# One-hot-like embedding products on one core: the x ring cut into 20 tiles, and loads of up to four tiles

## The chip, the core and the metric

One Trainium2 chip, one of its cores. The kernel is a single launch; the host only transposes and pads x, pads w and puts the output in order. The metric is device time in microseconds (us), the median of repeated runs. x is 104 MB of float32 and has to be read once, so bytes and the rate of the DMA engines are the first thing to look at.

## The reference

Ten tables, each a matrix product with a sparse x (float32, nearly all zeros, ones elsewhere), and a sum of them:

```python
VOCABS = [12500, 6250, 2500, 1250, 625, 250, 1000, 500, 200, 100]   # batch 1024, dim 64
embs = [jnp.dot(x, w) for x, w in zip(xs, ws)]
emb_sum = sum(embs)
q_emb = sum(jnp.dot(x ** 2, w ** 2) for x, w in zip(xs, ws))
fm_ans = 0.5 * (emb_sum ** 2 - q_emb)
return jnp.concatenate([fm_ans] + embs, axis=-1)
```

## The kernel before

A *tile* is 128 rows of the vocabulary by 1024 columns of the batch (512 KB). Partition p of a table holds consecutive rows of its vocabulary, so n neighbouring tiles are n x 4096 consecutive bytes of HBM for every partition, and n x 4096 bytes of SBUF. The last tile of a table (its *tail*) lies elsewhere and is loaded by itself. There are 203 tiles.

Tiles are worked through in *chunks* of one or two (`ORDER`, 108 chunks, numbered `k`), and chunks belong to *groups* of up to eight tiles (31 groups, numbered `g`), which share one load of weights. The tables come in the order 8, 9, 5, 4, 7, 3, 2, 1, 0, 6; tables 1 and 0 (49 and 98 tiles) are most of the work, and in them a group is four chunks of two tiles.

Each engine has its own instruction list, written out by hand, with semaphores between them:

- SP (`block.sync`) issues the loads of x into a ring of 8 slots (`SLOTS`) of two tiles each. The load of chunk k first waits until both readers have finished chunk k - 8 (`ones_counted` and `set_counted`). After the last x load it issues the stores of the results.
- DVE (`count_ones`) compares each chunk with 1 and counts the hits; nothing but a final check depends on the counts, but they hold the slot. Between chunks it adds a finished table's sums to `total` (`add(n)`, five chunks after the table's end), and that needs ACT's `copy_emb(n)`.
- ACT (`count_set`) makes `is_set`, the sign of each element, which is the matrix that TensorE multiplies, and counts as well. In the same list stand `load_w(g+3)`, a DMA of weights on ACT's own queue, issued in group g behind its second chunk; `square(g+2)`, which waits for those weights to land, behind the third chunk; and `copy_sums` and `copy_emb` for finished tables.
- POOL splits the weights into a high and a low part; PE multiplies each tile by both.

A weights load is 128 rows of up to 2048 bytes. Where a group holds the tail of a table whose tail is short (tables 8, 3, 2, 1, 0, 6), it is two or three DMAs, the extra ones with rows of 256 bytes.

Of the kernel before, what the change touches and what calls it, by code (L numbers as in the profile page):

```python
# [5 lines left out]
ALU = mybir.AluOpType  # L6
ACT = mybir.ActivationFunctionType
F32 = mybir.dt.float32
# [5 lines left out]
P = 128  # L14
D = 64
# [25 lines left out]
CHUNK = max(FULL)  # L41
GROUP = sum(FULL)

SLOTS = 8
SETS = 5

WHOLES = 3
# [8 lines left out]
class Chunk:  # L56


    def __init__(self, k, table, tile, n, at):
        self.k, self.table, self.tile, self.n, self.at = k, table, tile, n, at  # L60
        self.slot, self.turn = k % SLOTS, k // SLOTS
        self.tail = tile + n == TILES[table]

        self.rows = TAIL[table] if TILES[table] == 1 else P
        self.group = None


class Group:
# [31 lines left out]
NGROUPS, NCHUNKS = len(GROUPS), len(CHUNKS)  # L100


G_ORDER = [9] + [t for t in range(NT) if t != 9]
BEGIN = [min(g.chunks[0].k for g in GROUPS if g.place == n) for n in range(NT)]
END = [max(g.end for g in GROUPS if g.place == n) for n in range(NT)]
# [11 lines left out]
def rec_kernel(nc, xs, ws, out):  # L117
# [5 lines left out]
    with ExitStack() as ctx:  # L123
        def sb(name, shape, dt):
            return ctx.enter_context(nc.sbuf_tensor(name, shape, dt))
# [5 lines left out]

        sums = ctx.enter_context(nc.psum_tensor("sums", [P, NB, 512], F32))

        x_ring = sb("x_ring", [P, SLOTS * CHUNK * BATCH], F32)

        is_set = [sb(f"is_set{i}", [P, CHUNK * BATCH], F32R) for i in range(SETS)]
        is_one = [sb(f"is_one{i}", [P, CHUNK * BATCH], U8) for i in range(2)]
# [20 lines left out]
        g_weights = sb("g_weights", [P, 2, D], F32)  # L158

        w_landed = [sem(f"w_landed{i}") for i in range(WHOLES)]  # L160
        x_landed = [sem(f"x_landed{s}") for s in range(SLOTS)]
# [30 lines left out]

        block = ctx.enter_context(nc.Block())

        def in_slot(slot, elements):
            at = slot * CHUNK * BATCH
            return x_ring[:, at:at + elements]

        def x_of(chunk):
            return in_slot(chunk.slot, chunk.n * BATCH)[0:chunk.rows]  # L200

        def part_of(group, part):

# [13 lines left out]

        @block.sync
        def _(sp):
            for chunk in CHUNKS:  # L220
                if chunk.k >= SLOTS:

                    sp.wait_ge(ones_counted, chunk.k - SLOTS + 1)
                    sp.wait_ge(set_counted, chunk.k - SLOTS + 1)
                at = chunk.tile * BATCH
                sp.dma_start(x_of(chunk),
                             x_end[chunk.table] if chunk.tail else
                             x_dram[chunk.table][:, at:at + chunk.n * BATCH]
                             ).then_inc(x_landed[chunk.slot], 16)

            for n, (t, _) in enumerate(ORDER[:-1]):
                sp.wait_ge(emb_copied, n + 1)
                sp.dma_start(out[t + 1], results[:, t + 1, :, :]).then_inc(stored, 16)
            sp.wait_ge(fm_ready, 1)
            sp.dma_start(out[0], results[:, 0, :, :]).then_inc(stored, 16)
            sp.wait_ge(flag_ready, 1)
            odd = sp.value_load(odd_flag[0:1, 0:1], min_val=0, max_val=FLAG_MAX)
            sp.wait_ge(stored, 16 * (NT + 1))
            with sp.If(odd != 0):
                base = zeros = 0  # L240
                for t in G_ORDER:
                    end, rows = TILES[t] - 1, TAIL[t]
                    if end:
                        with sp.Fori(0, end) as i:

                            sp.wait_ge(g_multiplied, base + i + 1)
                            sp.dma_start(in_slot(0, BATCH), x_dram[t][:, bass.ds(i * BATCH, BATCH)]
                                         ).then_inc(gx_landed, 16)
# [3 lines left out]
                    sp.dma_start(in_slot(0, BATCH)[0:x_end[t].shape[0]], x_end[t]).then_inc(gx_landed, 16)  # L252
# [15 lines left out]
        def _(act):  # L268
# [20 lines left out]
                nc.scalar.activation(w[:, 1], w[:, 0], ACT.Square).then_inc(squared, 1)  # L289

            def count_set(chunk):
                act.wait_ge(x_landed[chunk.slot], 16 * (chunk.turn + 1))
                if chunk.k >= SETS:

                    act.wait_ge(x_multiplied, chunk.k - SETS + 1)
                nc.scalar.activation(  # L296
                    is_set[chunk.k % SETS][0:chunk.rows, 0:chunk.n * BATCH],
                    x_of(chunk).bitcast(U32), ACT.Sign,
                    accum_out=set_counts[0:chunk.rows, chunk.k:chunk.k + 1]).then_inc(set_counted, 1)
# [71 lines left out]
        def _(pe):  # L371
# [49 lines left out]
            with pe.If(odd != 0):  # L421
                with pe.Fori(0, sum(TILES)) as i:
                    pe.wait_ge(gx_landed, 16 * (i + 1))
                    pe.wait_ge(gw_landed, 16 * (i + 1))
                    pe.wait_ge(gx_ready, 2 * (i + 1))
                    for b in range(NB):
                        block_b = slice(b * P, (b + 1) * P)
                        nc.tensor.matmul(sums[:, b, 0:D], in_slot(0, BATCH)[:, block_b],
                                         g_weights[:, 0, :], start=True, stop=True,
                                         skip_group_check=True)  # L430
                        last = nc.tensor.matmul(sums[:, b, D:2 * D], in_slot(1, BATCH)[:, block_b],
                                                g_weights[:, 1, :], start=False, stop=True,
                                                skip_group_check=True)
                    last.then_inc(g_multiplied, 1)
# [3 lines left out]
        def _(dve):  # L438
# [4 lines left out]
            dve.wait_ge(constants, 4)  # L443

            def count_ones(chunk):
                dve.wait_ge(x_landed[chunk.slot], 16 * (chunk.turn + 1))
                if chunk.k >= 2:

                    dve.wait_ge(ones_counted, chunk.k - 1)
# [48 lines left out]
            with dve.If(odd != 0):  # L498
# [7 lines left out]
                dve.wait_ge(stored, 16 * (NT + 1))  # L506
                dve.wait_ge(x_multiplied, NCHUNKS)

                g_link(nc.vector.memset(in_slot(0, BATCH), 0.0))
                nc.vector.nop().then_inc(g_multiplied, 1)  # L510
                g_link(nc.vector.memset(total[:, :, :, :], 0.0))
                base = 0
                for t in G_ORDER:
# [3 lines left out]
                    def add_tile(i):  # L517
                        dve.wait_ge(gx_landed, 16 * (base + i + 1))
                        dve.wait_ge(gw_landed, 16 * (base + i + 1))
                        x, w = in_slot(0, BATCH), g_weights[:, 0, :]  # L520
                        nc.vector.tensor_tensor(in_slot(1, BATCH), x, x, ALU.mult
                                                ).then_inc(gx_ready, 1)
                        nc.vector.tensor_tensor(g_weights[:, 1, :], w, w, ALU.mult).then_inc(gx_ready, 1)
                        dve.wait_ge(g_multiplied, base + i + 2)
# [39 lines left out]
```

## Time and profile before

| | |
|---|---|
| time, median of 3 runs | 285.73 us (285.54 to 285.94) |
| the profiled execution's own time | 285.67 us |
| its span in the trace | 283.9 us |
| granted TensorE clock, mean | 0.987 |
| DVE busy | 240.3 us (85%) |
| ACT busy | 227.6 us (80%) |
| PE busy | 218.4 us (77%) |
| bytes moved by DMA | 113.88 MB, mean 401 GB/s |

The span runs from the first to the last instruction of the trace; 1.8 us of the measured time lie around it. Shares of busy time are averages over the whole span. "DMA share" in the trace is the mean busy share of the core's 16 DMA engines.

### The profile page before, as it was taken

How to read it: one execution, taken by the hardware profiler on the slowest of the kernel's cores; microseconds unless marked ns; L12 is line 12 of the kernel's file. 1: busy time of each engine (PE TensorE's matmuls, PEld its weight loads, DVE VectorE, ACT ScalarE, POOL GpSimd, SP SyncE). 2: the span in 40 equal slices, each digit the busy share in tenths (PEclk: the TensorE clock that was granted, in tenths of full speed). 3: DMA queues.
4: the chain of work that ended last, by engine and by line, in shares of the span. 5: the costliest groups of instructions: out<-in, count | busy, mean ns of one | idle time of the engine just before them, and what ended most of it. 6: DMA issues, size and time to landing. Idle time of an engine off the chain costs nothing.

```text
span 283.9 us, 2928 instructions
## 1 busy us (share of the span) xinstructions
PE 218.4 (77%) x878; PEld 154.2 (54%) x878; DVE 240.3 (85%) x236; ACT 227.6 (80%) x271; POOL 88.1 (31%) x68
## 2 busy tenths in 40 slices
PE   0459989998887878888687778778778778777791
PEld 0338657776565655555465555555555555545561
DVE  3752999999999989988789988988988988888874
ACT  0769999999978878878887877877877878778762
POOL 0432427317234124107244044044044044004000
PEclk9998999999999999999999999999999999999997
DMA  7999999999999999999999999999999999999972
GB/s 234 396 404 415 407 417 415 420 413 418 416 422 418 419 423 413 419 417 420 413 421 415 420 421 417 421 423 414 418 422 419 416 418 415 418 413 420 410 304 99
DMA packets 22417, 113.88 MB, mean 401 GB/s; under 512 B 3728, under 2 KB 4752, under 8 KB 10752
## 3 DMA queue, kind: packets, MB, share of 16 engines
q1 hardware_dynamic: 16976, 106.90, 91.5%
q10 hardware_dynamic: 5424, 6.79, 6.7%
q8 instruction: 7, 0.11, 0.2%
q14 instruction: 10, 0.08, 0.1%
HBM read 110.79 MB, written 2.88 MB: 400 GB/s over the span
## 4 chain that ended last, share of the span: by engine, by line
DMA 63%; issue 23%; DVE 6%; ACT 3%; PE 2%; POOL 1%; ACTq 1%; DVEq 0%; POOLq 0%
DMA x_ring<-in_x_dram 58%; DVE is_one L450 5%; DMA whole<-in_w_dram 5%; ACT is_set L296 2%; PE sums L385 1%; ACT turned L307 1%; POOL low L366 1%; PE sums L392 1%; DVE total L487 0%; ACT whole L289 0%; ACTq L276 0%; POOL high L364 0%; DVE results L490 0%; DVE results L493 0%; ACTq L283 0%
## 5 line engine op out<-in xcount | busy, mean ns | idle before, releaser
L450 DVE TENSOR_SCALAR_CACHE_REDUCE is_one<-x_ring 128x2048 uint8<-128x2048 f32 (+2 forms) x108 | 226.2, 2114 | 29.0 <-DMA x_ring<-in_x_dram 28.8
L296 ACT ACTIVATE is_set<-x_ring 128x2048 fp32r<-128x2048 uint32 (+2 forms) x108 | 192.2, 1784 | 37.2 <-DMA x_ring<-in_x_dram 37.1
L385 PE MATMUL sums<-is_set,low 128*128 128x512 f32 x398 | 134.8, 420 | 59.6 <-ACT is_set L296 52.7
L385 PE MATMUL sums<-is_set,high 128*128 128x512 f32 x398 | 125.9, 398 | 0.0
L385 PEld LDWEIGHTS sums<-is_set,low 128*128 128x128 f32 x398 | 68.4, 191 | 104.2 <-ACT is_set L296 54.3
L385 PEld LDWEIGHTS sums<-is_set,high 128*128 128x128 f32 x398 | 75.9, 191 | 17.5
L364 POOL CAST high<-whole 128x1024 fp32r<-128x1024 f32 (+5 forms) x31 | 27.0, 871 | 170.5 <-ACT whole L289 170.5
L366 POOL TENSOR_TENSOR low<-whole,high 128x1024 fp32r<-128x1024 f32 (+5 forms) x31 | 60.6, 1953 | 2.5
L296 ACT ACTIVATION_READ_ACCUMULATOR is_set<-x_ring 128x1 f32 (+1 forms) x108 | 20.7, 192 | 0.0
L289 ACT ACTIVATE whole<-whole 128x512 f32<-128x512 f32 (+5 forms) x31 | 16.8, 541 | 4.1 <-DMA whole<-in_w_dram 4.1
L392 PE MATMUL sums<-identity,turned 128*128 128x128 f32 x80 | 11.2, 286 | 0.8 <-ACT turned L337 0.8
L392 PEld LDWEIGHTS sums<-identity,turned 128*128 128x128 f32 x80 | 10.1, 150 | 2.6 <-issue 1.4
L462 DVE TENSOR_TENSOR total<-sums,total 128x1024 f32<-128x1024 f32 x8 | 9.7, 1219 | 1.7 <-ACT results L312 1.7
L307 ACT ACTIVATE turned<-sums 128x1024 f32<-128x1024 f32 x9 | 9.2, 1018 | 0.0
L450 DVE DVE_READ_ACCUMULATOR is_one<-x_ring 128x1 f32 (+1 forms) x108 | 8.8, 81 | 0.0
L459 DVE COPY total<-sums 128x1024 f32<-128x1024 f32 x1 | 1.2, 1225 | 8.2 <-ACT results L312 8.2
L289 ACT ACT_TABLE_LOAD x1 | 1.3, 1283 | 7.7 <-DMA whole<-in_w_dram 7.7
L312 ACT ACTIVATE results<-sums 128x512 f32<-128x512 f32 x9 | 5.4, 601 | 1.0 <-PE sums L392 1.0
L337 ACT ACTIVATE turned<-sums 128x512 f32<-128x512 f32 x2 | 1.1, 596 | 1.2 <-PE sums L385 1.2
L487 DVE TENSOR_TENSOR total<-sums,total 128x512 f32<-128x512 f32 x2 | 1.3, 685 | 0.9 <-PE sums L392 0.9
L342 ACT ACTIVATE results<-sums 128x256 f32<-128x256 f32 x2 | 0.8, 383 | 1.3 <-DVE total L487 1.3
L439 DVE MEMSET ones<- 128x128 f32 x1 | 0.2, 165 | 0.9 <-PEq L547 0.9
(17 smaller groups left out, 3.7 us busy)
## 6 DMA issues: line engine op xcount, KB each, us to landing
x_ring<-in_x_dram SPq DMA_DIRECT2D x91, 1024.0 KB, 18.3
x_ring<-in_x_dram SPq DMA_DIRECT2D x16, 512.0 KB, 10.2
whole<-in_w_dram ACTq DMA_DIRECT2D x19, 256.0 KB, 7.5
out_dram<-results SPq DMA_DIRECT2D x10, 256.0 KB, 12.4
x_ring<-in_x_dram SPq DMA_DIRECT2D x1, 448.0 KB, 6.5
whole<-in_w_dram ACTq DMA_DIRECT2D x2, 192.0 KB, 5.7
whole<-in_w_dram ACTq DMA_DIRECT2D x2, 160.0 KB, 7.2
out_dram<-results ACTq DMA_DIRECT2D x1, 256.0 KB, 2.1
```

The costliest lines, as they stand in the source:

```text
L289: nc.scalar.activation(w[:, 1], w[:, 0], ACT.Square).then_inc(squared, 1)
L296: nc.scalar.activation(is_set[chunk.k % SETS][0:chunk.rows, 0:chunk.n * BATCH], x_of(chunk).bitcast(U32), ACT.Sign, accum_out=set_counts[0 ...
L307: nc.scalar.activation(turned[n % 2][:, :].rearrange("p (a b) -> p a b", a=2), sums[:, at:at + 2, :], ACT.Copy).then_inc(sums_copied, 1)
L312: nc.scalar.activation(results[:, t + 1, :, :], turning(n)[:, :, 0, :], ACT.Copy).then_inc(emb_copied, 1)
L364: nc.gpsimd.tensor_copy(upper, w).then_inc(high_ready, 1)
L366: nc.gpsimd.tensor_tensor(part_of(group, low), w, upper.bitcast(F32), ALU.subtract).then_inc(parts_ready, 1)
L385: last = nc.tensor.matmul(sums[:, summing(n, half), :], w, x[0:chunk.rows, at:at + HALF], start=first, stop=False, skip_group_check=True)
L392: last = nc.tensor.transpose(turning(n)[:, b, :, :], turned[n % 2][:, b * P:(b + 1) * P], identity[:, :])
L450: nc.vector.tensor_scalar(is_one[chunk.k % 2][0:chunk.rows, 0:chunk.n * BATCH], x_of(chunk), 1.0, None, ALU.is_equal, ALU.add, accum_out=o ...
L459: nc.vector.tensor_copy(total[:, :, :, :], turning(n)).then_inc(added, 1)
L462: nc.vector.tensor_tensor(total[:, :, :, :], turning(n), total[:, :, :, :], ALU.add).then_inc(added, 1)
L487: nc.vector.tensor_tensor(total[:, blocks, :, :], turning(n)[:, blocks, :, :], total[:, blocks, :, :], ALU.add).then_inc(added, 1)
```

## The change

The ring becomes 20 tiles (`RING`) without slots, and a *load* becomes a thing of its own (`Load`, `plan_loads`). Neighbouring chunks of one group are joined into one load as long as it has at most four tiles (`LOAD`); a tail stays alone, and so do all chunks of the last table (`LAST`, table 6), whose loads are those of before. The load's place `at` runs around the ring, and jumps to 0 where the load wouldn't fit before the end. It waits (`free`) until the readers have finished every chunk whose place it overwrites. Semaphores for landing are 12 (`LANDS`) instead of 8. The readers still work chunk by chunk; both chunks of a load wait for the same landing. Of 64 loads, 42 have four tiles, 2 have three, 5 have two and 15 have one; before there were 108, 91 of two tiles and 17 of one.

```diff
-SLOTS = 8
+
+LOAD = 4
+RING = 20
+LANDS = 12
...
+def plan_loads():
+    lists = []
+    for group in GROUPS:
+        joined = []
+        for chunk in group.chunks:
+
+            if joined and (chunk.tail or group.table == LAST or sum(c.n for c in joined) + chunk.n > LOAD):
+                lists.append(joined)
+                joined = []
+            joined.append(chunk)
+        lists.append(joined)
+    loads, at = [], 0
+    for i, chunks in enumerate(lists):
+
+        at = 0 if at + sum(chunk.n for chunk in chunks) > RING else at
+        loads.append(Load(i, chunks, at))
+        at += loads[-1].n
+
+        loads[-1].free = max([o.end for o in loads[:-1] if o.at < at and loads[-1].at < o.at + o.n] +
+                             [o.end for o in loads[:-1] if o.land == loads[-1].land] + [0])
+    return loads
...
-        x_ring = sb("x_ring", [P, SLOTS * CHUNK * BATCH], F32)
+        x_ring = sb("x_ring", [P, RING * BATCH], F32)
...
-            for chunk in CHUNKS:
-                if chunk.k >= SLOTS:
-
-                    sp.wait_ge(ones_counted, chunk.k - SLOTS + 1)
-                    sp.wait_ge(set_counted, chunk.k - SLOTS + 1)
-                at = chunk.tile * BATCH
-                sp.dma_start(x_of(chunk),
-                             x_end[chunk.table] if chunk.tail else
-                             x_dram[chunk.table][:, at:at + chunk.n * BATCH]
-                             ).then_inc(x_landed[chunk.slot], 16)
+            free = 0
+            for load in LOADS:
+                if load.free > free:
+
+                    free = load.free
+                    sp.wait_ge(ones_counted, free)
+                    sp.wait_ge(set_counted, free)
+                at = load.tile * BATCH
+                sp.dma_start(in_ring(load.at, load.n)[0:load.rows],
+                             x_end[load.table] if load.tail else
+                             x_dram[load.table][:, at:at + load.n * BATCH]
+                             ).then_inc(x_landed[load.land], 16)
...
-                act.wait_ge(x_landed[chunk.slot], 16 * (chunk.turn + 1))
+                act.wait_ge(x_landed[chunk.load.land], 16 * (chunk.load.turn + 1))
...
-                dve.wait_ge(x_landed[chunk.slot], 16 * (chunk.turn + 1))
+                dve.wait_ge(x_landed[chunk.load.land], 16 * (chunk.load.turn + 1))
```

Only SP's list gets other instructions; the lists of ACT, DVE, PE and POOL keep theirs in the same order, with other landings to wait for.

SP's list at the start, before (in_x8 is x of table 8, and so on; 128x1024 is one tile, 128x2048 two; the times at the end count equal rows):

```order
L226 DMA x_ring<-in_x8_dram 128x1024 x2
L226 DMA x_ring<-in_x9_dram 112x1024
L226 DMA x_ring<-in_x5_dram 128x1024 x2
L226 DMA x_ring<-in_x4_dram 128x2048 x2
L226 DMA x_ring<-in_x4_dram 128x1024
L226 DMA x_ring<-in_x7_dram 128x2048 [waits set_counted,ones_counted]
L226 DMA x_ring<-in_x7_dram 128x1024 [waits set_counted,ones_counted] x2
```

The same place of the change:

```order
L268 DMA x_ring<-in_x8_dram 128x1024 x2
L268 DMA x_ring<-in_x9_dram 112x1024
L268 DMA x_ring<-in_x5_dram 128x1024 x2
L268 DMA x_ring<-in_x4_dram 128x4096
L268 DMA x_ring<-in_x4_dram 128x1024
L268 DMA x_ring<-in_x7_dram 128x3072
L268 DMA x_ring<-in_x7_dram 128x1024
L268 DMA x_ring<-in_x3_dram 128x4096
L268 DMA x_ring<-in_x3_dram 128x2048
L268 DMA x_ring<-in_x3_dram 128x3072 [waits set_counted,ones_counted]
```

Before, ten tiles are issued ahead of the first wait; now it is twenty, in eleven loads.

SP's list from table 2 to the end, before:

```order
L226 DMA x_ring<-in_x2_dram 128x2048 [waits set_counted,ones_counted] x9
L226 DMA x_ring<-in_x2_dram 128x1024 [waits set_counted,ones_counted] x2
L226 DMA x_ring<-in_x1_dram 128x2048 [waits set_counted,ones_counted] x24
L226 DMA x_ring<-in_x1_dram 128x1024 [waits set_counted,ones_counted]
L226 DMA x_ring<-in_x0_dram 128x2048 [waits set_counted,ones_counted] x48
L226 DMA x_ring<-in_x0_dram 128x1024 [waits set_counted,ones_counted] x2
L226 DMA x_ring<-in_x6_dram 128x2048 [waits set_counted,ones_counted] x3
L226 DMA x_ring<-in_x6_dram 128x1024 [waits set_counted,ones_counted] x2
```

And from table 1 to the end in the change:

```order
L268 DMA x_ring<-in_x1_dram 128x4096 [waits set_counted,ones_counted] x7
L268 DMA x_ring<-in_x1_dram 128x4096
L268 DMA x_ring<-in_x1_dram 128x4096 [waits set_counted,ones_counted] x4
L268 DMA x_ring<-in_x1_dram 128x1024 [waits set_counted,ones_counted]
L268 DMA x_ring<-in_x0_dram 128x4096 [waits set_counted,ones_counted] x24
L268 DMA x_ring<-in_x0_dram 128x1024 [waits set_counted,ones_counted]
L268 DMA x_ring<-in_x0_dram 128x1024
L268 DMA x_ring<-in_x6_dram 128x2048
L268 DMA x_ring<-in_x6_dram 128x2048 [waits set_counted,ones_counted]
L268 DMA x_ring<-in_x6_dram 128x2048
```

The 72 loads of two tiles of tables 1 and 0 have become 36 of four; the last table's are the same.

## Rows read from the trace of the kernel before

**Rows 1.** The page's second part: 40 equal slices of 7.1 us.

```profile
DMA  7999999999999999999999999999999999999972
GB/s 234 396 404 415 407 417 415 420 413 418 416 422 418 419 423 413 419 417 420 413 421 415 420 421 417 421 423 414 418 422 419 416 418 415 418 413 420 410 304 99
DMA packets 22417, 113.88 MB, mean 401 GB/s; under 512 B 3728, under 2 KB 4752, under 8 KB 10752
```

**Rows 2.** DMA queues (q1 SP's, q10 ACT's): packets, MB, share of 16 engines' span.

```profile
q1 hardware_dynamic: 16976, 106.90, 91.5%
q10 hardware_dynamic: 5424, 6.79, 6.7%
```

**Rows 3.** Windows: us, busy of PE, PEld, DVE, ACT, POOL, clock, DMA share, GB/s.

```profile
168.00:172.00 4.00, 3.01 (x12) 2.22 (x13) 3.62 (x5) 3.04 (x5) 0.00 (x0) 1.00 1.02 424
204.00:208.00 4.00, 3.16 (x13) 1.94 (x11) 3.54 (x3) 3.77 (x5) 1.98 (x2) 1.00 1.02 414
```

**Rows 4.** The page's groups: the two readers of x_ring.

```profile
L450 DVE TENSOR_SCALAR_CACHE_REDUCE is_one<-x_ring 128x2048 uint8<-128x2048 f32 (+2 forms) x108 | 226.2, 2114 | 29.0 <-DMA x_ring<-in_x_dram 28.8
L296 ACT ACTIVATE is_set<-x_ring 128x2048 fp32r<-128x2048 uint32 (+2 forms) x108 | 192.2, 1784 | 37.2 <-DMA x_ring<-in_x_dram 37.1
```

**Rows 5.** DMA issues: count, KB each, median us from issue to landing.

```profile
x_ring<-in_x_dram SPq DMA_DIRECT2D x91, 1024.0 KB, 18.3
whole<-in_w_dram ACTq DMA_DIRECT2D x19, 256.0 KB, 7.5
...
whole<-in_w_dram ACTq DMA_DIRECT2D x3, 28.0 KB, 9.1
```

**Rows 6.** Timeline of ACT in tables 0 and 6: start, us, what.

```profile
158.40 0.33 ACTq L276 DMA_DIRECT2D whole<-in_w_dram  x1
...
173.41 0.62 ACT L289 ACTIVATE whole<-whole 128x512 f32<-128x512 f32 x1
...
243.01 0.35 ACTq L276 DMA_DIRECT2D whole<-in_w_dram  x1
...
258.14 0.62 ACT L289 ACTIVATE whole<-whole 128x512 f32<-128x512 f32 x1
```

**Rows 7.** Timeline of ACT at the start: square(3) and its weights load, copy_emb(0).

```profile
10.65 0.33 ACTq L276 DMA_DIRECT2D whole<-in_w_dram  x1
...
17.00 0.47 ACT L289 ACTIVATE whole<-whole 128x320 f32<-128x320 f32 x1 [3.67 <-DMA whole<-in_w_dram]
...
26.26 0.59 ACT L312 ACTIVATE results<-sums 128x512 f32<-128x512 f32 x1
```

**Rows 8.** Timeline of DVE: add(0), and the chunk behind k = 22.

```profile
26.88 1.23 DVE L459 COPY total<-sums 128x1024 f32<-128x1024 f32 x1 [8.25 <-ACT results L312]
...
63.65 2.27 DVE L450 TENSOR_SCALAR_CACHE_REDUCE is_one<-x_ring 128x2048 uint8<-128x2048 f32 x1
```

**Rows 9.** Timeline of ACT at the end.

```profile
259.67 1.91 ACT L296 ACTIVATE is_set<-x_ring 128x2048 fp32r<-128x2048 uint32 x1 [0.91 <-DMA x_ring<-in_x_dram]
...
261.58 1.04 ACT L296 ACTIVATE is_set<-x_ring 128x1024 fp32r<-128x1024 uint32 x1
...
264.71 1.92 ACT L296 ACTIVATE is_set<-x_ring 128x2048 fp32r<-128x2048 uint32 x1 [0.96 <-DMA x_ring<-in_x_dram]
...
269.11 1.01 ACT L307 ACTIVATE turned<-sums 128x1024 f32<-128x1024 f32 x1
270.01 1.91 ACT L296 ACTIVATE is_set<-x_ring 128x2048 fp32r<-128x2048 uint32 x1
```

**Rows 10.** Timeline of DVE at the end.

```profile
269.68 2.29 DVE L450 TENSOR_SCALAR_CACHE_REDUCE is_one<-x_ring 128x2048 uint8<-128x2048 f32 x1 [0.19 <-DMA x_ring<-in_x_dram]
...
273.03 1.22 DVE L450 TENSOR_SCALAR_CACHE_REDUCE is_one<-x_ring 128x1024 uint8<-128x1024 f32 x1
...
275.71 1.22 DVE L462 TENSOR_TENSOR total<-sums,total 128x1024 f32<-128x1024 f32 x1 [1.45 <-ACT results L312]
```

More of the change, by code:

```diff
@@ L60, in __init__ @@
         self.k, self.table, self.tile, self.n, self.at = k, table, tile, n, at
-        self.slot, self.turn = k % SLOTS, k // SLOTS
         self.tail = tile + n == TILES[table]
         self.rows = TAIL[table] if TILES[table] == 1 else P
-        self.group = None
+        self.group = self.load = None
+class Load:
+    def __init__(self, i, chunks, at):
+        self.chunks, self.at, self.i = chunks, at, i
+        self.table, self.tile, self.tail = chunks[0].table, chunks[0].tile, chunks[0].tail
+        self.n, self.rows = sum(chunk.n for chunk in chunks), chunks[0].rows
+        self.end = chunks[-1].k + 1
+        self.land, self.turn = i % LANDS, i // LANDS
+        for chunk in chunks:
+            chunk.load, chunk.within = self, chunk.tile - self.tile
 class Group:
@@ L100 @@
 NGROUPS, NCHUNKS = len(GROUPS), len(CHUNKS)
+def plan_loads():
[16 more added lines that the diff above has]
+    return loads
+LOADS = plan_loads()
 G_ORDER = [9] + [t for t in range(NT) if t != 9]
@@ L160, in rec_kernel @@
         w_landed = [sem(f"w_landed{i}") for i in range(WHOLES)]
-        x_landed = [sem(f"x_landed{s}") for s in range(SLOTS)]
+        x_landed = [sem(f"x_landed{s}") for s in range(LANDS)]
         x_multiplied = sem("x_multiplied")
@@ L193, in rec_kernel, with in_ring @@
         block = ctx.enter_context(nc.Block())
-        def in_slot(slot, elements):
-            at = slot * CHUNK * BATCH
-            return x_ring[:, at:at + elements]
+        def in_ring(tile, n):
+            return x_ring[:, tile * BATCH:(tile + n) * BATCH]
         def x_of(chunk):
-            return in_slot(chunk.slot, chunk.n * BATCH)[0:chunk.rows]
+            return in_ring(chunk.load.at + chunk.within, chunk.n)[0:chunk.rows]
         def part_of(group, part):
@@ L246, in _ @@
                             sp.wait_ge(g_multiplied, base + i + 1)
-                            sp.dma_start(in_slot(0, BATCH), x_dram[t][:, bass.ds(i * BATCH, BATCH)]
+                            sp.dma_start(in_ring(0, 1), x_dram[t][:, bass.ds(i * BATCH, BATCH)]
                                          ).then_inc(gx_landed, 16)
@@ L251, in _ @@
                     sp.wait_ge(g_multiplied, base + end + 1)
-                    sp.dma_start(in_slot(0, BATCH)[0:x_end[t].shape[0]], x_end[t]).then_inc(gx_landed, 16)
+                    sp.dma_start(in_ring(0, 1)[0:x_end[t].shape[0]], x_end[t]).then_inc(gx_landed, 16)
                     w_end, before = w_dram[t][:, end * D:TILES[t] * D], P - rows if end else 0
@@ L427, in _ @@
                         block_b = slice(b * P, (b + 1) * P)
-                        nc.tensor.matmul(sums[:, b, 0:D], in_slot(0, BATCH)[:, block_b],
+                        nc.tensor.matmul(sums[:, b, 0:D], in_ring(0, 1)[:, block_b],
                                          g_weights[:, 0, :], start=True, stop=True,
                                          skip_group_check=True)
-                        last = nc.tensor.matmul(sums[:, b, D:2 * D], in_slot(1, BATCH)[:, block_b],
+                        last = nc.tensor.matmul(sums[:, b, D:2 * D], in_ring(1, 1)[:, block_b],
                                                 g_weights[:, 1, :], start=False, stop=True,
@@ L507, in _ @@
                 dve.wait_ge(x_multiplied, NCHUNKS)
-                g_link(nc.vector.memset(in_slot(0, BATCH), 0.0))
+                g_link(nc.vector.memset(in_ring(0, 1), 0.0))
                 nc.vector.nop().then_inc(g_multiplied, 1)
@@ L519, in add_tile @@
                         dve.wait_ge(gw_landed, 16 * (base + i + 1))
-                        x, w = in_slot(0, BATCH), g_weights[:, 0, :]
-                        nc.vector.tensor_tensor(in_slot(1, BATCH), x, x, ALU.mult
+                        x, w = in_ring(0, 1), g_weights[:, 0, :]
+                        nc.vector.tensor_tensor(in_ring(1, 1), x, x, ALU.mult
                                                 ).then_inc(gx_ready, 1)
```

## The prediction

> **What bounds the kernel now.** Read the slices first [rows 1]: from the second to the 38th the DMA engines are busy nine tenths or more, at 396 to 423 GB/s. Then the readers [rows 4]: DVE and ACT each sat idle before chunks, 29.0 and 37.2 us in all, and nearly all of it ended with a landing of x. So from about 7 us to about 270 us the DMA engines' rate sets the end, and some 12 us of closing work follow. No engine's busy share matters as long as x keeps streaming. Ahead of it lies a deep queue: a two-tile load lands 18.3 us after its issue [rows 5], though two tiles take only 1,048,576 B / 0.418 MB/us = 2.5 us at the rate of [rows 1].
>
> Two things can move the time: what a byte costs the DMA engines, and whether they ever run dry.
>
> **What a packet costs.** q1 has 16,976 packets [rows 2]. Counted from the code this is one per row and one per engine for each DMA's semaphore: 91 x 128 rows of 8 KB, 16 x 128 + 112 of 4 KB, 10 x 128 of stores, and 118 x 16 for semaphores. So a row of 8 KB is one packet. Solve the two queues for a price per packet a and per megabyte b, in engine-us out of 16 x 283.9 = 4542: q1 gives 16,976 a + 106.90 b = 0.915 x 4542 = 4156, q10 gives 5,424 a + 6.79 b = 0.067 x 4542 = 304. That is b = 37.4 us/MB (26.7 B/ns) and a = 9.2 ns. But the records overlap: the share reads 1.02 where an engine can't be over 1 [rows 3], and 2% of 4542 us over 22,417 packets [rows 1] is 4 ns each. So a packet costs between 5.2 and 9.2 ns beside its bytes.
>
> The change takes away 44 loads (108 less 64) and with each 128 rows and 16 semaphore packets: 44 x 144 = 6,336 packets, the bytes being the same. 6,336 x 5.2 / 16 = 2.1 us; x 9.2 = 3.6 us. I take 6.6 ns, nearer the lower end, since the overlap is real but its 4 ns comes from a share with two decimals: **-2.6 us**. The part of it after table 0 is nothing, so it is all there when the last table begins.
>
> The Trainium skill ("DMA: Bandwidth & Descriptors", Why small descriptors are slow) gives 3 cycles of overhead for each packet, at 850 MHz (same page, Where 436 GB/s comes from) 3.5 ns; by that, an estimate, the saving would be 1.4 us, and the packet's price in the rows is above it.
>
> **What the end costs.** The last load of table 0 before the tail's singles now lands two chunks at once, the earlier of them 2.5 us later than it would alone. Take its landing as time 0 (259.67 before) [rows 9]. The next arrivals are one 2-tile load at +5.04 (264.71), and +7.5 and +10.0 after it (269.68 on DVE) [rows 9, 10]. ACT has from time 0: 1.91 (first chunk), 0.5 (square(30), which stood ahead of the landing at 258.14 [rows 6] and now stands between the two), 1.91, 1.04 + 1.04: it is free at +6.4, not +4.0, so the 0.96 us of idle time before 264.71 is gone and ACT doesn't catch up: +8.3, +10.2, and 0.9 for copy_sums (269.11 to 270.01) gives +11.1 for the start of the third chunk, where before it was +10.34. That is **+0.8 us** on the path through ACT, PE and the closing copies. DVE is later by about 1.1 us (starts lie 0.08 us closer than the recorded 2.29 and 1.22, so two chunks of 2.21, two of 1.14, three of 2.21 and two of 1.14 make 15.6, against 14.5 from 259.67 to the end of its last count at 274.2), but it has 1.45 us of idle time before its add [rows 10]. Bounds: 0.4 if ACT recovers part of it, 1.4 if DVE's lag counts too.
>
> **Does the stream run dry?** SP waits for both readers of what a load overwrites. In table 0 the ring holds five four-tile loads, and the next is issued when the oldest pair of chunks is counted, so 16 tiles less those in work are queued: over 12 us. The tightest place by the plan is the second load of table 1 (load 21), which waits for chunk 22: 48 tiles are issued before it. DVE finishes chunk 22 at 63.65 [rows 8]. By then the first nine slices (63.9 us) have moved 3521 x 7.1 / 1000 = 25.0 MB [rows 1], less some 1.8 MB of weights (54 tiles of 32 KB): 44 tiles. Four tiles, 5 us, are still in the queue, 4 us after the time that a load needs to start. In this stretch both readers are behind (DVE sat 8.25 us before add(0) [rows 8], waiting for ACT's copy_emb(0) at 26.26, which was itself late because square(3) waited 3.67 us for weights [rows 7]). Whatever makes ACT later at the start moves 63.65 by as much. Cost taken: 0, with the cover of 4 us named.
>
> **Weights behind larger packets.** A 256 KB load of weights has 8 rows and a semaphore on each engine and takes 7.5 us [rows 5]; 9 x 0.09 us of its own would be below 1 us, so it alternates with x packets of 8 KB (0.31 us: 8192 B at 26.7 B/ns plus a), 9 x 0.31 = 2.8 us of it. With packets of 16 KB (0.62 us) this adds 2.8 us: 10.3 us. In table 0 it has 173.41 - 158.40 = 15.0 us [rows 6]: covered by 4.7 us. Where the load is three DMAs it has about 19 packets per engine and took 9.1 us [rows 5]: plus 19 x 0.31 = 5.9 makes 15.0, and it has 258.14 - 243.01 = 15.1 [rows 6]. That is the edge; ACT's list reaches load_w a little earlier when two chunks land together, about 2 us, which speaks for no stall. At the start, the load issued at 10.65 landed at 17.0 [rows 7]; at most 9 x 0.31 = 2.8 us more, less than the 4 us of cover. Cost taken: 0, at most 2.
>
> The skill's rule for it ("DMA: Bandwidth & Descriptors", Queues, rings and completion order) is that an engine goes round its queues and switches only at packet boundaries, so larger x packets hold weights up; the 7.5 us agree with alternation. It would turn the sum round only if both covers went, which is the third rival.
>
> **Sum.** 285.67 - 2.6 + 0.8 = **283.9 us**. The profiled execution lies 0.06 us under the median of the runs, so this stands for the median too.
>
> **Rivals.**
>
> 1. *Rows of 16 KB are cut back into packets of 8 KB or cost twice a packet's price.* Then only 44 x 16 semaphore packets go: 704 x 6.6 ns / 16 = 0.3 us. The end's 0.8 stays. 285.67 - 0.3 + 0.8 = **286.2 us**. Against it: a row of 8 KB is one packet where 4 KB rows are too [rows 2]; but no row shows 16 KB. The skill's "DMA: Bandwidth & Descriptors" (SWDGE vs HWDGE vs iDMA) prefers packets of at most 4096 B, which the 8 KB of this trace already exceed.
>
> 2. *The stream runs dry in tables 2 and 1.* ACT is made later at the start by slower weights (2.8 us for each of the loads for groups 3 and 4, some 5.6 together), copy_emb and with it DVE's add follow, chunk 22 is counted at 69 (63.65 + 5.6), load 21 comes some 1.5 us too late, and perhaps one more load as well. 1.5 to 4 us of idle DMA: 283.9 + 1.5 to 4, say **286.6 us**, slower. It decides from an ACT delay of 4 us on. For it: ACT and DVE have no idle time to catch up in here. Against: the x packets beside these first weights are in part 4 KB and 12 KB, and the ring reaches 20 tiles ahead, four to ten more than before at the start.
>
> 3. *Weights late at the table borders* (groups 9, 16, 29, 30): ACT stands 1 to 2 us in square(29) or square(30), shortly before the end, where it has 0.5 to 0.9 us of idle time per chunk to give. **284.9 us**.
>
> 4. *Packets cost the full 9.2 ns and the end nothing*: 285.67 - 3.6 + 0.4 = **282.5 us**.
>
> **How the numbers follow.** 0.2% of 285.7 is 0.57 us, about what a measurement of this kernel can tell. Forecast (282.7 to 284.9): 0.50. Rival 1: 0.18. Rival 2: 0.16. Rival 3: 0.10. Rival 4: 0.06. Faster by over 0.2% means under 285.2: forecast, rival 4 and half of rival 3, 0.61. Within 0.2%: most of rival 1, some of 2 and 3: 0.21. Slower, over 286.3: most of rival 2 and a third of rival 1: 0.18. The range of 282.6 to 286.7 takes in the ends of the packet price and rivals 1 to 3 up to their middles and leaves under 2 in 10 out.
>
> **What would show it.** In the page of the changed kernel: 22,417 - 6,336 = 16,081 packets, if rows of 16 KB are one packet (rival 1: 21,713 if cut in two). A rate of 424 GB/s in weights-free windows [rows 3] should become 427 to 428. The 256 KB weights should land after about 10.3 us. No slice between the second and the 38th should fall under 400 GB/s; a dip near 60 to 70 us is rival 2. At the end ACT should show no idle time before the last table's first chunk. The prediction is wrong if x arrives no faster, or if DMA engines stand idle.

## The result and the profile after

The changed kernel takes **282.47 us** (median of 4 runs, 282.42 to 282.64), the kernel before 285.84 us beside it (4 runs, 285.54 to 286.51). The ratio is 0.988, with a 95% interval of 0.9862 to 0.9898: faster, by 3.4 us. The prediction was 283.9 us with a range of 282.6 to 286.7, so the direction was right, but the time is 1.4 us lower than forecast and lies 0.1 us outside the range.

One number ahead of the prediction is wrong: there are 199 tiles (91 chunks of two and 17 of one), not 203. No step was worked out from it.

The page of the changed kernel, second and third part (slices of 7.0 us), which answer to [rows 1] and [rows 2]:

```profile
span 280.8 us, 2830 instructions
...
DMA  7999999999999999999999999999999999999972
GB/s 226 409 401 421 411 432 422 414 410 428 423 428 425 427 427 421 421 416 435 418 425 422 434 421 427 421 430 416 427 427 418 429 427 420 423 423 406 411 304 94
DMA packets 16080, 113.87 MB, mean 406 GB/s; under 512 B 3024, under 2 KB 4048, under 8 KB 9792
...
q1 hardware_dynamic: 10640, 106.89, 91.0%
```

The bytes are those of before, the packets are 6,337 fewer: a row of 16 KB is one packet. The DMA engines are still busy from the second slice to the 38th, and no slice lies under 400 GB/s. The kernel is bound as before; the same stream has become faster. One window over most of it, us, busy of PE, PEld, DVE, ACT, POOL, clock, DMA share, GB/s, first in the kernel before:

```profile
80.00:250.00 170.00, 135.67 (x522) 92.13 (x520) 150.44 (x133) 138.78 (x149) 53.85 (x35) 1.00 1.02 418
```

and in the changed kernel:

```profile
80.00:250.00 170.00, 134.06 (x537) 94.40 (x536) 149.20 (x134) 136.23 (x152) 55.43 (x35) 1.00 1.01 424
```

418 has become 424 GB/s. The readers' groups and the DMA issues, beside [rows 4, 5]:

```profile
L492 DVE TENSOR_SCALAR_CACHE_REDUCE is_one<-x_ring 128x2048 uint8<-128x2048 f32 (+2 forms) x108 | 223.6, 2115 | 30.5 <-DMA x_ring<-in_x_dram 30.3
...
L338 ACT ACTIVATE is_set<-x_ring 128x2048 fp32r<-128x2048 uint32 (+2 forms) x108 | 191.4, 1775 | 36.7 <-DMA x_ring<-in_x_dram 36.7
...
x_ring<-in_x_dram SPq DMA_DIRECT2D x42, 2048.0 KB, 21.0
...
whole<-in_w_dram ACTq DMA_DIRECT2D x19, 256.0 KB, 9.8
```

Both readers wait as long as before (DVE 29.0 before and 30.5 us now, ACT 37.2 and 36.7), only in fewer and longer pieces, and still for x. Weights land after 9.8 us instead of 7.5. In the waits of ACT (total, times, longest) this comes to almost nothing:

```profile
ACT is_set L338 <- DMA x_ring<-in_x_dram: 36.7, 36, 1.4
...
ACT whole L331 <- DMA whole<-in_w_dram: 4.7, 2, 4.2
```

4.7 us for weights in two waits, both in the early tables; the kernel before had 4.1 in two. Then ACT's timeline at the end, beside [rows 9]:

```profile
255.75 1.91 ACT L338 ACTIVATE is_set<-x_ring 128x2048 fp32r<-128x2048 uint32 x1 [1.39 <-DMA x_ring<-in_x_dram]
...
257.66 0.62 ACT L331 ACTIVATE whole<-whole 128x512 f32<-128x512 f32 x1
258.18 1.90 ACT L338 ACTIVATE is_set<-x_ring 128x2048 fp32r<-128x2048 uint32 x1
...
262.15 1.90 ACT L338 ACTIVATE is_set<-x_ring 128x2048 fp32r<-128x2048 uint32 x1
...
264.05 1.90 ACT L338 ACTIVATE is_set<-x_ring 128x2048 fp32r<-128x2048 uint32 x1
...
265.94 1.01 ACT L349 ACTIVATE turned<-sums 128x1024 f32<-128x1024 f32 x1
266.85 1.90 ACT L338 ACTIVATE is_set<-x_ring 128x2048 fp32r<-128x2048 uint32 x1
```

From the landing of the last pair of table 0 ACT works without a pause to the third chunk of the last table: 266.85 - 255.75 = 11.10 us, the +11.1 of the prediction. But the landing itself is 3.92 us earlier than before (259.67 - 255.75), where the saved packets were to make it 2.6. The third chunk starts 270.01 - 266.85 = 3.16 us earlier, and that is the gain of the profiled execution (285.67 - 282.5 = 3.17). So two questions are open: whether the packets are all of the gain, and where the 0.8 us of the end went.

### The profile page after: what moved, and what is told of

Read it like the earlier page. It is cut to its first block, busy times and chain, and to the rows that moved or that the text cites. A ratio compares the mean times of both kernels' runs of the same rounds, so it can differ in the third digit from the quotient of the medians.

```text
span 280.8 us, 2830 instructions
## 1 busy us (share of the span) xinstructions
PE 214.1 (76%) x878; PEld 154.2 (55%) x878; DVE 237.4 (85%) x236; ACT 224.1 (80%) x271; POOL 88.2 (31%) x68
## 4 chain that ended last, share of the span: by engine, by line
DMA 55%; issue 28%; DVE 7%; ACT 6%; PE 2%; ACTq 1%; DVEq 0%
DMA x_ring<-in_x_dram 50%; DVE is_one L492 6%; DMA whole<-in_w_dram 5%; ACT is_set L338 4%; PE sums L427 1%; ACT turned L349 1%; PE sums L434 1%; DVE total L529 0%; ACT whole L331 0%; ACTq L318 0%; ACT results L354 0%; ACTq L326 0%; DVE results L532 0%; DVE results L535 0%; ACT turned L379 0%
## 5 line engine op out<-in xcount | busy, mean ns | idle before, releaser
L492 DVE TENSOR_SCALAR_CACHE_REDUCE is_one<-x_ring 128x2048 uint8<-128x2048 f32 (+2 forms) x108 | 223.6, 2115 | 30.5 <-DMA x_ring<-in_x_dram 30.3
L338 ACT ACTIVATE is_set<-x_ring 128x2048 fp32r<-128x2048 uint32 (+2 forms) x108 | 191.4, 1775 | 36.7 <-DMA x_ring<-in_x_dram 36.7
L427 PE MATMUL sums<-is_set,low 128*128 128x512 f32 x398 | 133.2, 416 | 60.8 <-ACT is_set L338 53.3
L434 PE MATMUL sums<-identity,turned 128*128 128x128 f32 x80 | 10.6, 277 | 0.8 <-ACT turned L379 0.8
```

What stands on the lines that cost most here:

```text
L338: nc.scalar.activation(is_set[chunk.k % SETS][0:chunk.rows, 0:chunk.n * BATCH], x_of(chunk).bitcast(U32), ACT.Sign, accum_out=set_counts[0 ...
L427: last = nc.tensor.matmul(sums[:, summing(n, half), :], w, x[0:chunk.rows, at:at + HALF], start=first, stop=False, skip_group_check=True)
L434: last = nc.tensor.transpose(turning(n)[:, b, :, :], turned[n % 2][:, b * P:(b + 1) * P], identity[:, :])
L492: nc.vector.tensor_scalar(is_one[chunk.k % 2][0:chunk.rows, 0:chunk.n * BATCH], x_of(chunk), 1.0, None, ALU.is_equal, ALU.add, accum_out=o ...
```

## The experiments

The theory is that the packets are what was gained: each removed one was worth some 7.6 ns of one DMA engine. That figure is read off the packets' records: the bytes of 189 of the 199 tiles had been moved at 257.16 us before and at 254.15 in the changed kernel, 3.0 us earlier, and 3.0 x 16 / 6,337 = 7.6 ns. (The very last landing of x comes 3.2 us earlier, 268.94 instead of 272.15, which gives 8.1 ns.) The rivals are that the deeper ring does it (20 tiles instead of 8 slots, 21.0 us from issue to landing), and that landing and reading in pairs does.

**rows8k.** The plan, ring and landings of the change; each load is issued as DMAs of at most two tiles, so that rows are 8 KB again and readers still wait for the whole load (the counts that they wait for are adapted).

```diff
-                at = load.tile * BATCH
-                sp.dma_start(in_ring(load.at, load.n)[0:load.rows], ...
+                for piece in range(load.pieces):          # ceil(load.n / 2)
+                    n, at = min(2, load.n - 2 * piece), (load.tile + 2 * piece) * BATCH
+                    sp.dma_start(in_ring(load.at + 2 * piece, n)[0:load.rows], ...
```

> The changed kernel with every load of four or three tiles issued as two DMAs of up to two tiles each on the same landing semaphore, so that the readers still wait for all of it; ring, waits and landings are those of the change, the rows are 8 KB again. Theory A (the gain is the packets' price): the 44 x 128 = 5,632 row packets and 704 semaphore packets come back, the page counts about 22,420; with 8.1 ns each (3.2 us x 16 / 6,336, from the gain of the stream in the change) the time is 282.5 + 3.2 = 285.7 us, or more if the lag of landings is back as well (up to 286.6). Theory B (the gain is the deeper ring or fewer landings to wait for): it stays at about 282.5 us. Theory C (half of it each): 284 us.

**ring_only.** The ring of 20 tiles, without joining: `LOAD = 2`.

```diff
-LOAD = 4
+LOAD = 2
```

> The changed kernel with loads of at most two tiles: 108 loads with 8 KB rows as before, but in the ring of 20 tiles with 12 landings, so up to four tiles deeper. Theory A: the DMA engines were never short of work before, so depth gives nothing: 285.8 us, within 0.5. Theory B: the depth carries the gain: 282.5 to 283.5 us.

Measured: rows8k 285.72 us (12 runs), ratio 1.0004 (0.9996 to 1.0013); ring_only 285.57 us (11 runs), ratio 0.9998 (0.9989 to 1.0006). Both move as many packets as before. The page of rows8k:

```profile
span 284.0 us, 2874 instructions
...
DMA packets 22416, 113.87 MB, mean 401 GB/s; under 512 B 3728, under 2 KB 4752, under 8 KB 10752
...
whole<-in_w_dram ACTq DMA_DIRECT2D x19, 256.0 KB, 7.3
```

With everything of the change but its long rows, the gain is gone within what can be told (285.72 us, the kernel before 285.64 beside it), and the weights land as before. In ring_only x is issued 23.6 us ahead instead of 18.3 and arrives no faster: 418 GB/s from 80 to 250 us. Depth is worth nothing where the queue never emptied. These two kernels differ in the joined landing, and in that the ring is freed by up to four tiles at a time; both together cost 0.15 us, within what can be told.

**rows4k.** The other direction, in the kernel before: each two-tile load as two DMAs of one tile, rows of 4 KB.

```diff
-                sp.dma_start(x_of(chunk), ...
+                for piece in range(chunk.n):
+                    at = (chunk.tile + piece) * BATCH
+                    sp.dma_start(x_of(chunk)[:, piece * BATCH:(piece + 1) * BATCH], ...
```

> The kernel before with every two-tile load issued as two DMAs of one tile on the same semaphore: rows of 4 KB, 91 x 144 = 13,104 packets more. Theory A, a fixed price of 8.1 ns per packet: + 13,104 x 8.1 / 16 = 6.6 us, 292.4 us; with 5.2 ns, the lower bound of the prediction, 290.1; with 9.2 ns 293.4. Theory B, packets are free: 285.8 us. If the time rises by much more than 7 us, the price is not fixed per packet but grows in small ones, or the weights' packets, which now alternate with shorter ones, change something.

Measured: 292.14 us (4 runs), ratio 1.0225 (1.021 to 1.024), +6.5 us.

```profile
GB/s 227 386 401 401 405 403 403 409 408 407 405 410 408 407 410 403 408 409 407 405 410 405 407 409 409 405 410 406 407 410 408 407 410 402 405 406 408 410 314 106
DMA packets 35522, 113.89 MB, mean 392 GB/s; under 512 B 5185, under 2 KB 6209, under 8 KB 35505
...
whole<-in_w_dram ACTq DMA_DIRECT2D x19, 256.0 KB, 6.2
```

13,105 packets more for 6.5 us are 7.9 ns each; 6,337 less for 3.0 us are 7.6. A price per packet explains three row lengths: 4, 8 and 16 KB. By the times alone it could as well be a price per DMA, since every DMA of these runs that came or went had the same 144 packets (44 fewer for 3.0 us, 91 more for 6.5 us, some 70 ns each). The records of single packets tell the two apart: the median record of a row of x is 162 ns for 4 KB (rows4k), 314 for 8 (before) and 615 for 16 (the change). Doubling the row saves 2 x 162 - 314 = 10 and 2 x 314 - 615 = 13 ns, so the cost sits in the rows. That is above the prices measured by time, and records overlap: in each of these three traces the records between 80 and 250 us add up to 3.6 to 3.8 ns per packet more than 16 engines have in that time. The semaphore packets are counted at the same price; their own record is 9 ns. If they cost nothing, a row costs 8.5 to 8.9 ns. What in a packet takes the time, the engine or the memory, no run here separates.

**taper.** The end: the last full group of table 0 keeps its loads of two tiles, as before.

```diff
-sum(c.n for c in joined) + chunk.n > LOAD
+sum(c.n for c in joined) + chunk.n > (2 if group.g == NGROUPS - 3 else LOAD)
```

> The changed kernel with the last full group of table 0 in four loads of two tiles instead of two of four. Theory A (the end costs 0.8 us because the last two chunks of table 0 land together and ACT isn't free again before the end): 282.5 - 0.8 + 0.15 (288 packets more) = 281.8 us, and ACT waits for landings in the last table again, as the kernel before did. Theory B (the end is hidden, or lasts as long anyway): 282.5 to 282.7 us.

Measured: 282.60 us (4 runs), ratio 0.9892 (0.9877 to 0.9906): the same as the change, not 0.8 us less. ACT's timeline in taper:

```profile
255.68 1.92 ACT L338 ACTIVATE is_set<-x_ring 128x2048 fp32r<-128x2048 uint32 x1
...
261.66 1.91 ACT L338 ACTIVATE is_set<-x_ring 128x2048 fp32r<-128x2048 uint32 x1 [1.33 <-DMA x_ring<-in_x_dram]
...
264.14 1.91 ACT L338 ACTIVATE is_set<-x_ring 128x2048 fp32r<-128x2048 uint32 x1 [0.48 <-DMA x_ring<-in_x_dram]
...
266.05 1.01 ACT L349 ACTIVATE turned<-sums 128x1024 f32<-128x1024 f32 x1
266.96 1.90 ACT L338 ACTIVATE is_set<-x_ring 128x2048 fp32r<-128x2048 uint32 x1
```

The joined landing is undone: ACT waits again before both chunks of the last table (1.33 and 0.48 us), and its backlog is gone. Yet the third chunk starts at 266.96 instead of 266.85. The reason is in the distances between landings. Chunks of two tiles arrive every 2.5 us, but in each of these kernels one gap near 257 us is 0.7 to 0.95 us too long. Before it was the gap ahead of the last pair of table 0 (starts on DVE in the kernel before):

```profile
253.75 2.29 DVE L450 TENSOR_SCALAR_CACHE_REDUCE is_one<-x_ring 128x2048 uint8<-128x2048 f32 x1 [0.30 <-DMA x_ring<-in_x_dram]
...
256.23 2.29 DVE L450 TENSOR_SCALAR_CACHE_REDUCE is_one<-x_ring 128x2048 uint8<-128x2048 f32 x1 [0.19 <-DMA x_ring<-in_x_dram]
...
259.67 2.29 DVE L450 TENSOR_SCALAR_CACHE_REDUCE is_one<-x_ring 128x2048 uint8<-128x2048 f32 x1 [1.14 <-DMA x_ring<-in_x_dram]
```

256.23 - 253.75 = 2.48, then 259.67 - 256.23 = 3.44. The +5.04 of [rows 9] from there to the first pair of table 6 is an ordinary distance: two single tiles and a pair, four tiles at some 1.25 us each.

The trace has 16 steps of a semaphore for every load, which is one for each of the 16 DMA engines, and their times. These show what the long gap is. In the kernel before, the last two of the 16 steps of a landing lie 0.07 us apart at 256.21 (256.14 and 256.21) and 1.00 us apart at 259.64 (258.64 and 259.64), and they stay 1.0 us apart in every landing to the end. This reads as one engine that falls a microsecond behind once, near 257 us, and doesn't catch up; a landing needs all 16, so this one and all later ones are late. In the changed kernel the same step falls later in the order of the loads: the last four tiles of table 0 land at 255.72 with the last two steps 0.11 us apart, and the second single tile behind them at 258.98 with 1.02 us. From the pair to the first landing of table 6 (261.47) it is 5.75 us instead of 5.04; in taper 5.98 (255.66 to 261.64).

So ACT has 0.7 us more to finish table 0, and its backlog is nearly gone by the second pair of table 6: that lands at 263.95 and ACT takes it at 264.05, 0.10 us late. From this landing to the third chunk it is 266.85 - 263.95 = 2.90 us in the change, 2.83 before (267.18 to 270.01) and 2.84 in taper (264.12 to 266.96). The joined landing costs 0.07 us, and in taper the 288 packets that come back (0.15 us by the expectation, 0.17 between the landings at 261.64 and 261.47) outweigh it. What makes the engine late is argued, not shown: between 254 and 260 us each of these traces has one or two packets of an instruction queue (in the kernel before "q14 instruction: 2, 0.02, 0.7%" of that window), of 8 KB each and 0.31 to 0.36 us long, which is less than the delay.

**last_joined.** The other side of the change: the last table joined too.

```diff
-if joined and (chunk.tail or group.table == LAST or sum(c.n for c in joined) + chunk.n > LOAD):
+if joined and (chunk.tail or sum(c.n for c in joined) + chunk.n > LOAD):
```

> The changed kernel with the last table's chunks joined like all others (loads of 4, 3 and the tail). One theory: its second and third loads land 2.5 us later for their first chunks, ACT, which has caught up by the second chunk of this table in the change, falls behind by 1 to 1.5 us before the closing copies, less 0.15 us for 288 packets: 283.4 us. Rival: that is hidden as the pairs of table 0 were (282.5 us).

Measured: 284.09 us (6 runs), ratio 0.9951 (0.9939 to 0.9963), about 1.6 to 2 us slower than the change. Its ACT timeline:

```profile
263.38 1.91 ACT L338 ACTIVATE is_set<-x_ring 128x2048 fp32r<-128x2048 uint32 x1 [1.65 <-DMA x_ring<-in_x_dram]
...
265.30 1.90 ACT L338 ACTIVATE is_set<-x_ring 128x2048 fp32r<-128x2048 uint32 x1
...
268.09 1.90 ACT L338 ACTIVATE is_set<-x_ring 128x2048 fp32r<-128x2048 uint32 x1
```

Here the first pair waits for the second, ACT sits idle for 1.65 us and then has both to do, and the third chunk starts at 268.09, 1.24 us later than in the change; ACT's copy of the sums then waits 1.58 us for PE instead of 1.00, and DVE's last add starts at 274.38 instead of 272.56. That is more than the first theory's 283.4 us: the wait for PE was not in it. Behind the last load no later work absorbs a delay. Joining everything would have kept only some 40% of the gain (1.3 of 3.4 us).

**ring16.** Is the cover of 4 us against a dry stream real? `RING = 16`, the tiles that the eight slots of before held.

```diff
-RING = 20
+RING = 16
```

> The changed kernel with a ring of 16 tiles, as much x as before the change. In table 0 four loads lie in it, and a new one is issued when the oldest is counted, with 12 tiles less those in work still queued: over 9 us. If depth is not needed: 282.5 us. Theory B (the tables before need it): loads of up to four tiles wait for whole old loads, at the start 5 us of cover shrink to none, and the DMA engines run dry once or more: 283.5 to 286 us, with slices under 400 GB/s between 20 and 80 us.

Measured: 285.26 us (10 runs, 284.43 to 286.68), ratio 0.9997 (0.9982 to 1.0011). The gain is gone:

```profile
span 282.7 us, 2831 instructions
...
DMA  7999999999999999999999999999999999999982
GB/s 225 415 395 416 418 350 388 421 388 435 425 433 417 431 425 419 424 431 421 416 429 417 427 423 433 423 425 421 423 427 427 428 427 419 420 422 404 413 313 96
```

The sixth to the ninth slice (35 to 64 us) hold 350, 388, 421, 388 GB/s where the change has 432, 422, 414, 410, and behind them the rate is that of the change. This is rival 2's mechanism: DVE and ACT are behind in tables 3 to 1, and SP can't issue four tiles before the oldest pair of chunks is read (the longest wait of SP for ACT is 13.5 us, against 7.0 in the change). The load issued at 36.39 us comes 1.5 us before the one ahead of it has landed (37.87). Its first packets start at 37.34 and take 0.9 to 1.5 us each instead of 0.62, and the DMA share of 38 to 40 us falls to 0.83. In the change the smallest such distance is 6.4 us, at load 21, where the prediction looked for it (issued at 64.29, the load ahead landed at 70.70). The profiled execution (284.43) is the fastest of the ten, so the rows show less of it than the median. So the 20 tiles are half of the change: useless by themselves, and what lets the joined loads keep their gain.

**load8, ctl_small, load8_rows16.** One step further: loads of up to eight tiles, rows of 32 KB, in a ring of 24. To make room for it, `SETS` is 4 and `PAIRS` 3; ctl_small changes these two alone. The last two groups ahead of table 6 keep loads of four and of two.

```diff
-LOAD = 4
-RING = 20
-SETS = 5
-PAIRS = 4
+LOAD = 8
+RING = 24
+SETS = 4
+PAIRS = 3
```

> Rows of 32 KB: loads of up to eight tiles, table 0's last two groups in loads of four and two, ring of 24 tiles; room for it from 4 instead of 5 buffers for is_set and 3 instead of 4 pairs of weights. Theory A (8.0 ns per packet whatever its size, weights still in time): 46 loads instead of 64 are 2,592 packets fewer, 2,592 x 8 / 16 = 1.3 us, 281.2 us. Theory B (weights behind 32 KB packets): the weights' 256 KB landed after 6.2, 7.4 and 9.8 us with x rows of 4, 8 and 16 KB, so 9.8 + 4.8 = 14.6 us here, where some 15 us are to be had: ACT waits in square, DVE and the ring follow, 283 us or more. Theory C (rows of 32 KB are cut in two): packets as in the change, 282.5 us.

> The changed kernel with 4 instead of 5 buffers for is_set and 3 instead of 4 pairs of weights, all else as it is: the control for the eight-tile loads. PE reads is_set within 2 us of its landing and ACT writes one in 2.5 us, so nothing should wait: 282.5 us; if it is slower, by so much the eight-tile loads are to be read better.

Measured: ctl_small 282.32 us (4 runs), ratio 0.9884 (0.9869 to 0.9899), the same as the change. load8 290.59 us (5 runs), ratio 1.0182 (1.0163 to 1.0202), slower than both kernels although it has the fewest packets of all. Its page:

```profile
GB/s 239 428 391 429 459 391 426 430 265 365 272 447 435 390 458 436 401 436 384 405 411 350 428 310 430 422 458 395 449 418 428 447 406 422 411 409 415 415 338 111
DMA packets 13488, 113.87 MB, mean 394 GB/s; under 512 B 2736, under 2 KB 3760, under 8 KB 9376
...
whole<-in_w_dram ACTq DMA_DIRECT2D x19, 256.0 KB, 13.1
```

and the longest of ACT's waits for weights in it:

```profile
62.52 0.52 ACT L331 ACTIVATE whole<-whole 128x384 f32<-128x384 f32 x1 [5.58 <-DMA whole<-in_w_dram]
```

Weights need 13.1 us, ACT stands 16.2 us for them in seven waits, and each time it holds the places that SP needs: slices of 265, 272 and 310 GB/s. Two things are mixed here, rows that hold up the weights, and a ring that is freed eight tiles at a time. load8_rows16 keeps the plan of load8 and issues each load as DMAs of at most four tiles:

```diff
-                sp.dma_start(in_ring(load.at, load.n)[0:load.rows], ...
+                for piece in range(load.pieces):          # ceil(load.n / 4)
+                    n, at = min(4, load.n - 4 * piece), (load.tile + 4 * piece) * BATCH
+                    sp.dma_start(in_ring(load.at + 4 * piece, n)[0:load.rows], ...
```

> The kernel with loads of up to eight tiles (290.6 us), each issued as DMAs of at most four tiles on one landing semaphore: rows of 16 KB, packets nearly as in the change, but readers and ring still go by eight tiles. If the weights' landing behind 32 KB packets cost it 8 us (13.1 us instead of 9.8, and 5.6 us of ACT's idle time in one place), the time comes back to 282.5 to 283.5 us and the weights land after 9.8 us. If it is the coarse ring, whose next load waits for eight tiles to be read, it stays at 288 to 291 us with the same dips of the DMA rate.

Measured: 284.81 us (10 runs), ratio 0.9985 (0.9972 to 0.9997), weights 9.8 us. By the ratios, of the 3.0% between ctl_small and load8 the coarser ring takes 1.0% (2.9 us: slices of 392, 355 and 359 GB/s remain in the middle, and ACT waits for x up to 5.1 us at a time) and the rows of 32 KB take 2.0% (5.6 us). The time lies between the two theories, nearer to the first. The granted clock is lower too, 0.93 in load8 and 0.95 in load8_rows16 where ctl_small has 0.98 (in load8 it is 0.79 from 64 to 72 us, behind 8 us in which PE was busy for 3.3); whether that costs time of its own is not separated.

**quarters, halves.** These were to price the semaphore packets and the DMAs themselves: the rows of the change, but each load as four DMAs of 32 partitions, or two of 64.

```diff
-                sp.dma_start(in_ring(load.at, load.n)[0:load.rows], ...
+                for part in range(load.parts):            # quarters 4, halves 2
+                    r = load.rows // load.parts
+                    rows = slice(part * r, (part + 1) * r)
+                    sp.dma_start(in_ring(load.at, load.n)[rows], ...
```

> The changed kernel with each load issued as four DMAs of 32 partitions on one landing semaphore: the same rows of the same sizes, but 63 x 3 x 16 = 3,024 semaphore packets more. If a semaphore packet costs what a row's packet costs (8.0 ns): + 1.5 us, 284.0 us. If it is free and only rows count: 282.5 us. Much more than 284 would mean that a DMA has a price of its own, beyond its packets.

> The changed kernel with each load issued as two DMAs of 64 partitions. With four DMAs of 32 partitions the rate fell from 423 to 217 GB/s and a 16 KB packet took 1.22 instead of 0.62 us. If the partitions that a DMA spans decide (fewer of them, fewer ways into SBUF at a time), 64 partitions should lie between or keep the full rate: 283 us at full rate (1,008 packets more, 0.5 us), or some 400 to 520 us.

Measured: quarters 520.8 us (4 runs, 504 to 528), halves 525.83 us (one run). The page of halves:

```profile
GB/s 209 215 232 209 237 215 216 218 228 216 210 216 216 212 218 213 216 216 218 216 214 215 220 214 211 220 216 211 214 217 213 218 214 217 215 218 214 226 228 230
DMA packets 17089, 113.87 MB, mean 217 GB/s; under 512 B 4033, under 2 KB 5057, under 8 KB 10801
```

The same rows, 1,009 packets more, and half the rate all through, with the DMA engines shown as busy: a packet of 16 KB takes 1.22 us in both where it takes 0.62. From 100 to 400 us both kernels move 215 GB/s, although quarters has twice as many DMAs, so it isn't a price per DMA or per packet. Neither kernel could price a semaphore packet; by time it stays unmeasured.

## Why the prediction was right in direction and short in size

- **What bounds the kernel**: right. rows8k differs from the change, and rows4k from the kernel before, in nothing but how x is cut into rows and DMAs, and the time follows both ways.
- **Packet price, -2.6 us**: the mechanism was right and the term was sized too small. It was bracketed at 5.2 to 9.2 ns and taken as 6.6; it measured 7.6 to 8.1 (change) and 7.9 ns (rows4k), -3.0 to -3.2 us. The correction of 4 ns for overlapping records was about right (3.7 in the kernel before). What was low is the 9.2 from solving the two queues, which takes both at one price per byte and per packet: the records of x alone give 10 to 13 ns. The middle of the bracket, 7.2, would have been nearer than the argued value. The 3.5 ns that an estimate by the Trainium skill gave ("DMA: Bandwidth & Descriptors", Why small descriptors are slow) doesn't hold here: by it the change gains 1.4 us and rows4k loses 2.9, and 3.0 and 6.5 were measured.
- **The end, +0.8 us**: this is the step that failed; 0.07 us were measured (the working stands under taper). Its reckoning from the landing on came out: ACT's with 11.10 us, and DVE's to a tenth (its last count ends at 271.42, 15.7 us after the landing, against 15.6). What was wrong is "The next arrivals are one 2-tile load at +5.04 (264.71)": it took the distances between landings as fixed. One engine's delay of 1 us near 257 us lay ahead of that landing before and lies behind it now, so the distance is 5.75, and the joined pair nearly fits in. That is luck: with 5.04 again, ACT's 11.10 us would have cost the 0.8 that was forecast, and nothing in the trace of before could tell that the delay would stay at its time while the stream moved. In the sum: -3.23 us for the landing of the last table's second pair (267.18 to 263.95, the packets), +0.07 for the end, -3.16 us. The forecast was -1.8; of what it missed, 0.6 us are the packets' and 0.7 the end's.
- **Stream runs dry, 0**: right, and the cover is real but thin: 6.4 us at load 21. With 16 tiles instead of 20 it is gone (ring16, +2.8 us). The start went as feared, only small: square(3) waits 4.15 us instead of 3.67 and DVE's add(0) starts at 27.42 instead of 26.88.
- **Weights, 0 at most 2**: right. 9.8 us where 10.3 was predicted, and 6.2, 7.5, 9.8 and 13.1 us with rows of 4, 8, 16 and 32 KB. The traces show the alternation itself: the packets of one 256 KB load start over 2.1 us in rows4k, 3.8 before and 5.8 in the change. For 32 KB it says 9.8 + 9 x (1.21 - 0.62) = 15.1 us, more than the 13.1 measured. The load of three DMAs was the edge that the prediction saw: it was issued at 240.00 and its last part landed at 255.76, 14.9 us after that part's own issue (15.0 were forecast), and square(30) ran at 257.66. What kept 1.9 us of cover (4.9 before: 253.26 and 258.14) is that ACT reached load_w 17.7 us ahead of square(30) instead of 15.1. Longer waits for weights came only with rows of 32 KB.
- **Rate**: 427 to 428 GB/s were forecast for windows without weights; such windows hold 403 to 427, scattered by where packets end, so that sign was too fine to read. Over 170 us it is 418 to 424.
- **Rivals**: 1 is refuted by the packet count. 2 and 3 did not happen in the change: no slice from the second to the 38th is under 400 GB/s, and ACT's two waits for weights are early ones. Rival 4 named 282.5 us, which is what came out, but by another split: 9.2 ns and an end of +0.4, where it was 7.6 to 8.1 ns and an end of +0.1.

No version tried is clearly faster than the change; ctl_small's 282.32 us can't be told from 282.47.

## What to carry to other kernels

When DMA engines are busy all through and bytes can't be cut, count packets: here each cost 7.6 to 8 ns of one engine, so that rows of 16 KB instead of 8 gave 1.1% (against rows8k), and rows of 4 KB cost 2.3%. Longer rows are paid for elsewhere: other queues' transfers wait behind them (weights 9.8 us at 16 KB, 13.1 at 32 KB), the ring has to be deeper by what is freed later, and the last loads of all stay short. Before reckoning from one landing, look at the distances between several: one that is too long is a delay, and a change that moves the stream can put it on the other side of the landing. A term of the size of such a delay is not safe from one trace.

## What the runs showed of the hardware that was not expected

- A load cut into DMAs of 64 or 32 partitions ran at 217 GB/s instead of 424, with the same rows and bytes and DMA engines shown as busy throughout; a 16 KB packet took 1.22 us instead of 0.62. Why, no run here shows.
- In the three traces compared (before, change, taper) one of the 16 steps of a landing falls 1.0 us behind the others near 257 us, at a fixed time and not at a fixed chunk, and stays behind to the end; the gap between two landings grows once by 0.7 to 0.95 us.
